# Eight logit columns carried by four gate units, the sigmoid ahead of two weight splits, and the rank product one unit earlier, in a gated mixture-of-experts block

## The reference, cut to what matters

```python
x = x + jnp.tanh(g_xattn[0]) * _L0_xattn_ref(_layernorm(x), fside, ctx_1024)
h = _layernorm(x)                                  # 1,024 tokens, 256 features
conf = sigmoid(einsum('bsh,eh->bse', h, conf_W) + conf_b)      # 8 logits a token
bids = conf * expert_wealth
top_bids, sel = top_k(bids, 2);  routing = softmax(top_bids)
base_g = h @ base_gate;  base_u = h @ base_up      # 896 columns each, same for all experts
for e in range(8):                                  # only the 2 chosen ones count
    g = base_g + h @ gate_A[e] @ gate_B[e] * 0.25
    u = base_u + h @ up_A[e] @ up_B[e] * 0.25
    a = silu(g) * u
    out += we[e] * (a @ base_down + a @ down_A[e] @ down_B[e] * 0.25)
x = x + jnp.tanh(g_ffn[0]) * out
```

## Time and profile before

| | us |
|---|---|
| median of 3 runs | 305.18 |
| lowest and highest | 304.8 and 308.1 |
| span of the profiled execution | 303.4 |
| PE, DVE, ACT, POOL busy in it | 256.1, 196.5, 158.1, 121.6 |

### The profile page before, as it was taken

How to read it: one execution, slowest core, us unless ns; L and a number is a source line. 1 busy time by engine, 2 the same in 40 slices (tenths; PEclk the granted TensorE clock), 3 DMA queues, 4 the chain that set the end, 5 groups by cost and what they waited for, 6 DMA issues and landing times.

```text
span 303.4 us, 5240 instructions
## 1 busy us (share of the span) xinstructions
PE 256.1 (84%) x1577; PEld 235.1 (77%) x1578; DVE 196.5 (65%) x412; ACT 158.1 (52%) x285; POOL 121.6 (40%) x145
## 2 busy tenths in 40 slices
PE   0756576999999998999999999999999999998400
PEld 0646464889798887999999999999999999988400
DVE  2968889786359313876666677766666677763134
ACT  3336978987664336555554445555454445551011
POOL 4478557649652113233234444333334444110211
PEclk9978697799999999999999999999999999998955
DMA  6952523468989353444444333444444343400074
GB/s 170 299 151 66 137 68 93 120 220 249 304 266 316 142 199 117 162 146 150 138 158 149 104 110 139 156 138 147 147 156 144 96 125 136 138 17 2 35 247 168
DMA packets 31342, 45.69 MB, mean 151 GB/s; under 512 B 14104, under 2 KB 25760, under 8 KB 31328
## 3 DMA queue, kind: packets, MB, share of 16 engines
q0 software_dynamic: 4416, 21.50, 21.4%
q1 hardware_dynamic: 20752, 14.03, 16.7%
q10 hardware_dynamic: 6160, 9.98, 9.3%
HBM read 33.57 MB, written 11.93 MB: 150 GB/s over the span
## 4 chain that ended last, share of the span: by engine, by line
PE 66%; DVE 15%; DMA 8%; ACT 4%; issue 3%; POOL 2%; SPq 1%; ACTq 0%; DVEq 0%
PE pY L55 9%; PE pY L59 8%; PE pY L57 8%; PE pT L1544 5%; PE pG L55 4%; PE pG L57 3%; PE pG L59 3%; PE pU L57 3%; PE pU L59 3%; PE pU L55 3%; DMA x_resid<-in_x_dram 2%; PE bank L55 2%; PE bank L59 2%; PE bank L57 2%; DMA yr<-results 2%
## 5 line engine op out<-in xcount | busy, mean ns | idle before, releaser
L507 POOL DMA_INDIRECT results<-yb,dest x19 | 18.7, 986 | 93.2 <-DVE yb L1180 93.2
L55 PE MATMUL pY<-Wd_hi,hT_hi 128*128 128x384 f32 x126 | 45.1, 358 | 0.2 <-issue 0.2
L59 PE MATMUL pY<-Wd_hi,hT_lo 128*128 128x384 f32 x126 | 42.4, 336 | 0.0
L57 PE MATMUL pY<-Wd_lo,hT_hi 128*128 128x384 f32 x126 | 42.3, 336 | 0.0
L742 ACT CAST xaT_hi<-pX 128x256 fp32r<-128x256 f32 x19 | 7.1, 373 | 46.5 <-PE pX L1519 46.5
L501 POOL DMA_INDIRECT bin<-base_products,tok x18 | 22.0, 1221 | 17.1 <-issue 7.9
L493 POOL DMA_INDIRECT xin<-normed,tok x19 | 18.6, 979 | 23.2 <-PE pX L1505 9.7
L766 ACT CAST hT_hi<-pT 128x896 fp32r<-128x896 f32 x19 | 17.2, 907 | 18.5 <-PE pT L1544 18.5
L55 PE MATMUL bank<-Wbase_hi,x2T_hi 128*128 128x448 f32 x64 | 24.6, 384 | 0.7 <-ACT brow L635 0.7
L55 PEld LDWEIGHTS pY<-Wd_hi,hT_hi 128*128 128x128 f32 x126 | 23.7, 188 | 1.7 <-issue 0.8
L57 PEld LDWEIGHTS pY<-Wd_lo,hT_hi 128*128 128x128 f32 x126 | 23.8, 189 | 0.0
(11 more groups left out here) (256 smaller groups left out, 735.7 us busy)
## 6 DMA issues: line engine op xcount, KB each, us to landing
base_products<-brow ACTq DMA_DIRECT2D x16, 448.0 KB, 3.4
yr<-results SPq DMA_DIRECT2D x8, 256.0 KB, 5.1
raw<-in_L_ffn_gate_B_dram SPq DMA_DIRECT2D x8, 224.0 KB, 2.6
raw<-in_L_ffn_up_B_dram SPq DMA_DIRECT2D x8, 224.0 KB, 3.2
raw<-in_L_ffn_down_A_dram SPq DMA_DIRECT2D x7, 256.0 KB, 4.8
x_resid<-in_x_dram SPq DMA_DIRECT2D x4, 256.0 KB, 5.4
q<-in_fside_BxS2xS_dram ACTq DMA_DIRECT2D x4, 256.0 KB, 7.0
normed<-q ACTq DMA_DIRECT2D x4, 256.0 KB, 3.9
```

Source lines behind the costliest of these rows:

```text
L55: m.matmul(outs[i], hi, whi[i], start=first, stop=False, skip_group_check=True)
L57: m.matmul(outs[i], hi, wlo[i], start=False, stop=False, skip_group_check=True)
L59: ins = m.matmul(outs[i], lo, whi[i], start=False, stop=last, skip_group_check=True)
L507: g.indirect_dma_start(out=yg, out_offset=bass.IndirectOffsetOnAxis(ap=dest[:, j:j + 1], axis=0), in_=yb[:, :], in_offset=None).then_inc(d ...
```

## The change

Three things are changed, and a fourth goes with them.

1. The first four token tiles (`EARLY = 4`) have no logit matmuls of their own. The eight columns of the logit weights stand behind the 896 columns of the gate weights (`Wbase_hi` and `Wbase_lo` are 904 columns wide), and the second gate unit of each of these tiles is 128x456 in place of 128x448. ACT copies these 8 columns to `early` ahead of its copy to `brow`; DVE adds the bias in two instructions, for the late tiles out of bank A[1] and for the early ones out of `early`, after it has waited for the copy of unit 11 (`EARLY_LAST`). `logits(0)` and `logits(1)` are gone.
2. The units of tiles 2 and 3 stand in another order (gate of tile 2, gate of tile 3, up of tile 2, up of tile 3), so that the last early logits come out of unit 11. On PE x2_T(3) stands behind unit 9, logits(2) behind unit 10, logits(3) behind unit 11. On ACT the sigmoid stands behind the output of unit 11 and ahead of the two weight splits that stood before it.
3. The rank product stands behind unit 16, not 17.
4. `attile`, a small table of the place chain, lies in another piece of memory.

```diff
@@ memory
-        Wbase_hi = sb("Wbase_hi", [P, 2, HC, I], F32R, base_scope)
-        Wbase_lo = sb("Wbase_lo", [P, 2, HC, I], F32R, base_scope)
+        Wbase_hi = sb("Wbase_hi", [P, 2, HC, I + E], F32R, base_scope)
+        Wbase_lo = sb("Wbase_lo", [P, 2, HC, I + E], F32R, base_scope)
-            cWT_hi = s1("cWT_hi", [P, HC, E], F32R)
-            cWT_lo = s1("cWT_lo", [P, HC, E], F32R)
+            cWT_hi, cWT_lo = Wbase_hi[:, 0, :, I:I + E], Wbase_lo[:, 0, :, I:I + E]
+            early = s1("early", [P, EARLY, E])
-            attile = s1("attile", [P, NG, PT])
+                attile = sb("attile", [P, NG, PT], F32, quant)
@@ unit order
+        UNIT_ORDER = [(t, gu) for t in range(TB) for gu in range(2)] + [(t, gu) for gu in range(2) for t in range(TB, EARLY)] \
+            + [(t, gu) for t in range(EARLY, NT) for gu in range(2)]
+        EARLY_LAST = 2 * UNIT_ORDER.index((EARLY - 1, 0)) + 1
+        def unit_cols(u):
+            t, gu, i = unit_of(u)
+            return IH + (E if gu == 0 and i == 1 and t < EARLY else 0)
@@ ACT, unit_out
+                if unit_cols(u) > IH:
+                    a.copy(early[:, t, :], unit_bank(u)[:, IH:IH + E])
                 a.copy(brow[:, k % 3, i * IH:(i + 1) * IH], unit_bank(u)[:, 0:IH]).then_inc(s_copied, 1)
@@ ACT, order
             unit_out(7)
+            unit_out(8)
             resid(3)
             split(1)
             x2_hi(3)
+            unit_out(9)
             split(1)
-            unit_out(8)
-            unit_out(9)
-            split(2)
+            unit_out(10)
+            unit_out(11)
             act.wait_ge(s_logit, 1)
             a.activation(bids[:, :, :], bids[:, :, :], ACT.Sigmoid).then_inc(s_sig, 1)
-            for u in range(10, 13):
-                unit_out(u)
+            split(2)
+            unit_out(12)
@@ DVE
-            v.tensor_tensor(bids[:, :, :], A[1][:, 0:NT * E].rearrange("p (t e) -> p t e", t=NT), row(0), ALU.add).then_inc(s_logit, 1)
+            v.tensor_tensor(bids[:, EARLY:NT, :], A[1][:, EARLY * E:NT * E].rearrange("p (t e) -> p t e", t=NT - EARLY), row(0)[:, EARLY:NT], ALU.add)
+            dve.wait_ge(s_copied, EARLY_LAST + 1)
+            v.tensor_tensor(bids[:, 0:EARLY, :], early[:, :, :], row(0)[:, 0:EARLY], ALU.add).then_inc(s_logit, 1)
@@ PE, unit
+                if u == 1:
+                    pe.wait_ge(s_cWT, 1)
+                w = slice(i * IH, i * IH + unit_cols(u))
@@ PE, order
             q2_T(3)
-            logits(0)
             products2(3)
             row_c(3)
             unit(5)
-            logits(1)
             x2_T(2)
             unit(6)
             unit(7)
-            logits(2)
-            x2_T(3)
             unit(8)
             unit(9)
+            x2_T(3)
+            unit(10)
+            logits(2)
+            unit(11)
             logits(3)
-            for u in range(10, 18):
+            for u in range(12, 17):
                 unit(u)
             ...
-            for u in range(18, 24):
+            for u in range(17, 24):
                 unit(u)
```

More of the change, by code:

```diff
@@ L84, in build @@
     assert PT % 2 == 1
+    EARLY = 4
     assert TB == 2 and HC == 2 and I2 == P and ER == 512 and IH <= 512 and fside.shape[1] == S
@@ L349, in build @@
             landed.append((landed[n - RING] if n >= RING else 0) + 16 * len(chunks[n][0]))
-        PRE = NT - 2
+        UNIT_ORDER = [(t, gu) for t in range(TB) for gu in range(2)] + [(t, gu) for gu in range(2) for t in range(TB, EARLY)] \
[4 more added lines that the diff above has]
+            return IH + (E if gu == 0 and i == 1 and t < EARLY else 0)
         def results(b, k):
@@ L358, in unit_of @@
         def unit_of(u):
-            return u // 4, (u // 2) % 2, u % 2
+            t, gu = UNIT_ORDER[u // 2]
+            return t, gu, u % 2
         def unit_bank(u):
@@ L958, in cW_out @@
                 pc = A[3][:, 0:HC * E].rearrange("p (c e) -> p c e", c=HC)
-                link(v.tensor_copy(cWT_hi[:, :, :], pc))
-                v.tensor_tensor(cWT_lo[:, :, :], pc, cWT_hi[:, :, :], ALU.subtract).then_inc(s_cWT, 1)
+                link(v.tensor_copy(cWT_hi, pc))
+                v.tensor_tensor(cWT_lo, pc, cWT_hi, ALU.subtract).then_inc(s_cWT, 1)
             stats(0)
@@ L1389, in unit @@
                         pe.wait_ge(s_wlo, 2 * (gu * HC + c) + i + 1)
-                    ins = split_product([unit_bank(u)[:, 0:IH]], x2T_hi[:, b, c, q], x2T_lo[:, b, c, q],
-                                        [Wbase_hi[:, gu, c, i * IH:(i + 1) * IH]], [Wbase_lo[:, gu, c, i * IH:(i + 1) * IH]],
-                                        c == 0, c == HC - 1)
+                    ins = split_product([unit_bank(u)[:, 0:unit_cols(u)]], x2T_hi[:, b, c, q], x2T_lo[:, b, c, q],
+                                        [Wbase_hi[:, gu, c, w]], [Wbase_lo[:, gu, c, w]], c == 0, c == HC - 1)
                 ins.then_inc(s_made, 1)
```

## The result

The median of 20 runs is 307.01 us (304.66 to 309.05), of the kernel before 304.95 us: 2.06 us more. The ratio is 1.0099, 95% interval 1.0072 to 1.0125, so the kernel is slower by about 1%, 3 us by this ratio and 2 by the medians. The two differ because every ratio here leaves out a kernel's slow executions, those more than 1.5% above its fastest: four of the 20 of the kernel before and none of the changed kernel's, and further on 5 of 12 for the sigmoid alone and 4 of 12 for the first combined version, whose profiled executions were both among the slow ones. The forecast was 304.9 us, the range ended at 306.6, and "slower by over 1%" had a chance of 0.04.

What follows compares the result with a forecast made beforehand. PE was taken to bound the kernel (84% busy, 66% of the chain). Of at most 3.99 us, waits and a later pick chain left 0.3 us gain at x_T(0): 305.18 becomes 304.9 us, range 302.3 to 306.6.

Steps and rivals of the forecast that it cites:

- products2(3), x2_T(2), units 8 and 9: On PE, idle of about 1 us ahead of products2(3) and of x2_T(2); unit 8 at 73.05, unit 9 at 74.75.
- Rival B: PE is not held by the norm chain and the whole 3.99 us come: 301.2 us; chance 0.12.
- The late logits and the sigmoid: logits(3) ends at 81.6, unit 12 gains 0.8 us; the sigmoid ends at 82.45, half a microsecond later.
- The pick chain and the two splits: DVE chain behind the sigmoid: 3.7 us plus three POOL meetings of 1.0 us; pickb at 89.2, between 88.2 and 90.2.
- Rival A: The pick chain's meetings with POOL are no more than before: 1.9 us gained at x_T(0), 303.3 us; chance 0.25.
- The rank product's wait: PE has done units 12 to 16 at 87.8 and stands until pickb, 89.2, in place of 89.83.
- the signs of being wrong: x2_T(2) before 69.8, rank product without wait, sigmoid near 80, or granted clock under 1.00 between 62 and 110 us.
- Rival C: Clock falls at two new 1.0 us PE holes near 66.4 and 69.3: 307.9 us; chance 0.08, smaller loss 0.03.
- the hole at 82.41: PE's 0.73 us wait ahead of unit 12 in the kernel before, for an ACT copy; the clock did not fall there.
- 107.9 to 108.5: Forecast start of x_T(0), the first transpose of the expert tiles on PE, in us, against 108.39 before.
- The sort product: Place chain done at 98.3, so PE's 0.75 us wait there is gone; a third meeting makes it 99.3.

Runs made afterwards that it cites:

- the sigmoid alone: Kernel before with only the sigmoid moved ahead of the two weight splits on ACT; ratio 0.9997 to the kernel before.
- the first combined version: Changed kernel with POOL's low parts held back, splits ahead of unit 11's output and the sigmoid, unit 6 ahead of x2_T(2); ratio 0.9932 to the kernel before.
- filler: Changed kernel with 12 unread 128x448 matmuls on PE ahead of the rank product; ratio 1.0037 to the kernel before.
- products later: Changed kernel with the rank product behind unit 18 and the sort product behind unit 25, two units later each; ratio 1.0004 to the kernel before.
- rank product behind 17: Changed kernel with the rank product one unit later, behind unit 17 as before, sort product unmoved; ratio 1.003 to the kernel before.
- the run with the next splits one output later: Changed kernel with the two splits ahead of unit 11's output and the sigmoid, later splits one unit output later; ratio 1.0003 to the kernel before.
- the kernel before with more low parts: Kernel before with three more unread 128x512 POOL subtractions behind the sigmoid and the rank product behind unit 16; ratio 1.0100 to the kernel before.
- low parts held back: Changed kernel with POOL's last seven low-part subtractions held until the place chain is done, their splits moved behind; ratio 0.9988 to the kernel before.
- the run with the splits first: Changed kernel with one weight split ahead of unit 11's output and the other ahead of the sigmoid; ratio 1.0048 to the kernel before.

## Why the prediction was wrong

Times of the trace after are put at the place of the trace before by taking off the 0.67 us of x2_T(1).

- **products2(3), x2_T(2), units 8 and 9: right.** Idle of 0.78 and 0.81 us ahead of the two, as forecast near 1; q2T and the norm hold PE. Unit 9 stands at 75.30 - 0.67 = 74.63, forecast 74.75. Rival B falls: most of the 2.60 us of the logits ended in waits.
- **The late logits and the sigmoid: right.** Unit 12 stands at 82.12 - 0.67 = 81.45 (forecast 81.6), the sigmoid ends at 82.22 (82.45). "Ahead of the splits" made it no earlier than 81.94, because its input came later.
- **The pick chain and the two splits: the mechanism right, the term mis-sized.** "I take three meetings (two are certain by this, four possible)" gave 3.7 + 3 x 1.0 = 6.7 us. It was five, 8.0 us from the sigmoid's end to `pickb`, which is 1.3 more; 0.2 comes off for the earlier sigmoid, and the rank product stands at 90.32 in place of 89.2. I had counted the two splits behind the sigmoid and one more. But each meeting lengthens the chain by 0.9 and so keeps it under the next subtraction: POOL had five in 83.47 to 90.23, and the chain got out only when POOL was through. Rival A, fewer meetings, had a chance of 0.25; nothing in this trace bears it out.
- **The rank product's wait: the step that failed.** I gave it 1.4 us (87.8 to 89.2) and priced it as idle time alone; what the clock does behind it I put at nothing, without a reason. It was 2.52, and the clock fell to 0.50 behind it: 1.2 to 1.5 us. Of the signs of being wrong one came, a granted clock under 1.00 between 62 and 110 us. Rival C held this mechanism, with its price, at the two 1 us holes near 66 and 69 us, where the clock stayed at 1.00; its own bound, "the hole at 82.41 did not do it", spoke for those. The longest hole of my own forecast I did not put to it. Rival C's 307.9 us lies near the measured time, but by another hole than the one that did it. In the sum, 107.9 to 108.5 plus 1.1 plus 1.3 is 110.3 to 110.9, and x_T(0) stands at 111.24 - 0.67 = 110.57.
- **The sort product: right.** Its 0.75 us wait is gone. That was the gain of the earlier rank product, and it was smaller than the unit given for it.
- **The rest of the 3 us.** 2.05 us are accounted for at the first expert tile. The ratio says 3.0 (2.2 to 3.8), the medians of all 20 executions 2.06. Behind that tile the two orders are the same, the profiled executions differ by 0.5, and runs of one kernel differ by more (the 20 runs of before spread from 302.2 to 308.1, for which the last section shows one source). Whether anything beyond the 2.05 is left to explain stays open.

Lateness and clock are shown singly (filler, products later, rank product behind 17), and the meetings as the cause of the long wait from both sides: held back in the changed kernel, added in the kernel before. The Trainium skill, page "SBUF — State Buffer", section "Who interferes with whom", has a reduction never contending with GpSimd on this chip; the 0.22 us reductions under POOL's subtractions agree.

## What to carry to other kernels

Before a chain of small VectorE instructions is moved, lay it on the timeline of GpSimd, and count each GpSimd instruction that it can reach, including those that it reaches only because earlier meetings made it longer. Put every wait that a change lengthens to the clock as well, the longest one first: ask what PE runs just behind it, and what it costs at half the clock. And an earlier input to PE is worth something only where PE would stand for it; here the sigmoid 2 us earlier changed nothing while PE had its units up to 17 to do.

## What the runs showed of the hardware

- **A small VectorE instruction under a GpSimd subtraction** took 0.91 to 1.33 us in place of about 0.2 where it met most of one subtraction of about 1.3 us, at every size seen: 128x64, a 128x8 difference (1.14), a 128x4 copy (1.22), a cast to bf16 (1.02). Reductions of 128x64 kept their 0.22 us, and one instruction with its input in PSUM, at 90.25 us of the run with the next splits one output later, took 0.16 under a subtraction. Where subtractions stood back to back, one such instruction got through at each boundary: five in the changed kernel, eight in the kernel before with more low parts.
- **The clock behind a wait.** It stayed at 1.00 behind single waits of 0.78, 0.81 and 1.34 us, and went to 0.50 behind 1.87, 2.52 and 4.11 us. It was low as well behind two waits of 0.67 and 0.46 us close together, and once with no wait in the 6 us ahead of it (the run with the next splits one output later). These are single executions, so they give no limit. In the one execution that was profiled of it, two units' worth of idle matmuls ahead of the rank product kept the clock at 1.00 and delayed nothing.
- **The same wait, with and without a low clock.** In the last expert tile every one of the 14 traces has a wait of 1.08 us for ACT's `hT_hi`. In five of them (before, changed, low parts held back, sigmoid alone, first combined version) the clock fell to 0.50 within 3 us behind it, in the other nine it stayed at 1.00 up to the next wait, with traces of the old and of the new order on both sides. PE and its stretches, of the changed kernel and then of the run with the splits first:

```profile
280.09 1.08 PE L1589 MATMUL pU<-WdA_hi,hT_hi 128*128 x7 [1.08 <-ACT hT_hi L778]
...
282.00:284.00 2.00, 2.00 (x12) 2.00 (x12) 0.30 (x2) 0.00 (x0) 0.00 (x0) 0.52 0.03 8
```

```profile
278.12 1.08 PE L1590 MATMUL pU<-WdA_hi,hT_hi 128*128 x7 [1.08 <-ACT hT_hi L779]
...
280.00:282.00 2.00, 2.00 (x19) 2.00 (x19) 0.72 (x2) 0.00 (x0) 0.09 (x1) 1.00 0.04 8
```

PE's next wait comes 7.99 us behind this row in the changed kernel and 6.44 in the other run, so the low clock cost 1.5 us; it was low for longer in the sigmoid-alone run and the first combined version and cost 3.1 there (9.71 and 9.51 us; the kernels of the old order have 6.6 without it). The part behind the first hidden transpose took 181.2 to 181.8 us in the nine traces without it and 182.6, 183.1, 184.0, 184.2 and 185.9 in the five with it. For two of them, low parts held back and the first combined version, that is about 1 us more than the price of the low clock, which I can't explain. So a single profiled span can hide or feign 1.5 to 3 us by this alone, and a change this small is read from stretches ahead of that part and from many runs.
